# Group averages on the vector engine by 32x32 block transposes, from the fourth sample on

## The reference

```
# per sample; x, ctx: 256 x 1024; 8 groups of 32 rows ("GROUPS = 8", cg = 32)
t = Wt @ ctx;  p = Wp @ layernorm(x);  g = Wg @ ctx
att = sum over each group (32 rows x 1024) of p * g          # one number per group
y  = Wz_group @ (att * t)                                    # per group, 32 x 32
yn = (y - mean(y)) * rsqrt(var(y) + 1e-5)                    # mean, var over the group
x  = x + tanh(g_xattn) * (yn * gn_w + gn_b + ctx)
# feed-forward: h = layernorm(x)
scores = (h @ Wq^T) @ keys^T                                 # 64 experts, rank 8 each
gate   = softmax over the 16 largest scores, 0 elsewhere
out    = ((h @ A^T) * gate, each gate over 8 columns) @ B^T * 2
x      = x + tanh(g_ffn) * out
```

## Time and profile before

| | us |
|---|---|
| median of 3 runs | 324.51 (324.15 to 326.56) |
| the profiled execution, its own time | 325.73 |
| its span, first to last instruction | 323.9 |
| PE busy | 319.0 (98%) |
| DVE busy | 245.9 (76%) |
| ACT busy | 174.9 (54%) |
| POOL busy | 168.5 (52%) |
| mean granted clock of TensorE | 0.995 of full |

### The profile page before, as it was taken

How to read it: one execution, slowest core, us unless ns; L and a number is a source line. 1 busy time by engine, 2 the same in 40 slices (tenths; PEclk the granted TensorE clock), 3 DMA queues, 4 the chain that set the end, 5 groups by cost and what they waited for, 6 DMA issues and landing times.

```text
span 323.9 us, 5543 instructions
## 1 busy us (share of the span) xinstructions
PE 319.0 (98%) x1960; PEld 290.4 (90%) x1960; DVE 245.9 (76%) x636; ACT 174.9 (54%) x298; POOL 168.5 (52%) x158
## 2 busy tenths in 40 slices
PE   8999999999999999999999999999999999999996
PEld 6688998899988999898999899898999889989985
DVE  1856897596588946888887799788987798789362
ACT  3687845677256485286545658177454654354110
POOL 0464699189463969339581677429591580010000
PEclk9998999999999999999999999999999999999999
DMA  7999900990650585249951899228961631272102
GB/s 248 412 388 397 363 4 7 328 306 10 191 200 13 184 300 190 63 134 272 405 200 34 253 358 361 67 89 275 365 252 61 224 134 74 58 244 82 65 32 99
DMA packets 28091, 62.69 MB, mean 194 GB/s; under 512 B 2448, under 2 KB 12560, under 8 KB 28064
## 3 DMA queue, kind: packets, MB, share of 16 engines
q1 hardware_dynamic: 27712, 62.14, 54.6%
q10 hardware_dynamic: 352, 0.20, 0.2%
HBM read 46.34 MB, written 15.99 MB: 192 GB/s over the span
## 4 chain that ended last, share of the span: by engine, by line
PE 94%; DMA 3%; SPq 1%; issue 0%; ACT 0%; DVE 0%
PE z_ps L1266 20%; PE w_ps L1296 18%; PE w_ps L1185 12%; PE w_ps L1266 12%; PE z_ps L1125 9%; PE w_ps L1303 9%; PE z_ps L1104 4%; DMA cT_first<-in_cT 3%; PE t_ps L1213 2%; PE w_ps L1125 2%; PE t_ps L1243 2%; PE t_ps L1280 1%; PE z_ps L1198 1%; PE z_ps L1213 1%; PE t_ps L1342 1%; PE w_ps L1314 0%
## 5 line engine op out<-in xcount | busy, mean ns | idle before, releaser
L1296 PE MATMUL w_ps<-B_hi,zT_hi 128*128 128x512 f32 x124 | 49.3, 397 | 0.0
L1296 PE MATMUL w_ps<-B_lo,zT_hi 128*128 128x512 f32 x124 | 48.4, 391 | 0.0
L384 POOL TENSOR_TENSOR xT_lo<-xT_in,xT_hi 128x512 fp32r<-128x512 f32 x24 | 30.6, 1298 | 20.5 <-ACT xT_hi L500 17.7
L418 POOL TENSOR_TENSOR c_sb<-c_sb,x_sb 128x512 f32<-128x512 f32 x28 | 36.2, 1329 | 6.9 <-ACT c_sb L603 6.9
L403 POOL TENSOR_TENSOR c_lo<-c_sb,c_hi 128x512 fp32r<-128x512 f32 x24 | 30.3, 1292 | 14.1 <-DVE uw L863 14.1
L557 ACT ACTIVATE uw<-w_ps,neg_u 128x512 f32<-128x512 f32 x32 | 20.2, 686 | 28.8 <-DVE neg_u L808 28.8
L574 ACT ACTIVATE hT_hi<-t_ps 128x512 fp32r<-128x512 f32 x32 | 18.5, 599 | 30.7 <-DVE t_ps L884 22.5
L1266 PE MATMUL z_ps<-A_hi,hT_hi 128*128 128x288 f32 x160 | 34.7, 298 | 0.2 <-ACT hT_hi L574 0.2
L1266 PE MATMUL z_ps<-A_lo,hT_hi 128*128 128x288 f32 x160 | 34.1, 294 | 0.0
L1303 PE MATMUL w_ps<-B_hi,zT_lo 128*128 128x512 f32 x124 | 33.3, 390 | 0.0
L384 POOL TENSOR_TENSOR cT_lo<-cT_in,cT_hi 128x512 fp32r<-128x512 f32 x24 | 30.6, 1300 | 2.4 <-DVE uw L863 2.4
(11 more groups left out here) (191 smaller groups left out, 846.8 us busy)
## 6 DMA issues: line engine op xcount, KB each, us to landing
c_sb<-in_ctx SPq DMA_DIRECT2D x16, 512.0 KB, 6.8
x_sb<-in_x SPq DMA_DIRECT2D x16, 512.0 KB, 7.3
xT_in<-in_xT SPq DMA_DIRECT2D x14, 512.0 KB, 6.8
cT_in<-in_cT SPq DMA_DIRECT2D x14, 512.0 KB, 8.1
out_block<-uw SPq DMA_DIRECT2D x14, 512.0 KB, 6.2
w_through<-uw SPq DMA_DIRECT2D x10, 512.0 KB, 3.2
c_sb<-w_through SPq DMA_DIRECT2D x10, 512.0 KB, 4.0
z_through<-zg_sb SPq DMA_DIRECT2D x9, 256.0 KB, 2.3
```

What stands on the lines that cost most here:

```text
L384: last = pool.tensor_tensor(lo[:, chunks, :], came[:, chunks, :], hi[:, chunks, :].bitcast(f32), ALU.subtract)
L418: last = pool.tensor_tensor(c_sb[n % 2][:, t, cols], c_sb[n % 2][:, t, cols], x_sb[:, t, cols], ALU.add)
L1296: pe.matmul(w_ps[k][:, :], zT_hi[:, t, row], w[:, j, cols], start=(j == 0 and w is B_hi), stop=False)
```

## The change

For samples 0 to 2 nothing changes in the order of the work. From sample 3 on (samples 3 to 7) both averages over the groups are made on DVE, by a new helper of three instructions, each waiting for the one before: a transpose of a 128x32 tile in blocks of 32x32, so that each group's 32 values of one column lie along one row; a product with ones and 1/32 with a running sum, which leaves the average of each row in one column; and a transpose of that column, read 32 times over, which puts it back into all rows of the group. The inputs `u_mv` and `att_var` become the first columns of zeroed 128x32 tiles. The ten small products on PE, the copy of their result out of PSUM, and PE's waits for them are gone.

```diff
+        u_block, att_block = sb("u_block", [P, GROUP]), sb("att_block", [P, GROUP])
+        u_mv = u_block[:, 0:2 * T].rearrange("p (t k) -> p t k", k=2)
+        turned_in, turned_out, ones = sb("turned_in", [P, GROUP]), sb("turned_out", [P, GROUP]), sb("ones", [P, GROUP])
+        group_avg = sb("group_avg", [P, 1])
-        att_var, va = sb("att_var", [P, 2 * T]), sb("va", [P, 2 * T])
+        att_var, va = att_block[:, 0:2 * T], sb("va", [P, 2 * T])
...
+            def averages(block):
+                step(dve.transpose(turned_in[:, :], block[:, :]))
+                settle()
+                step(dve.scalar_tensor_tensor(turned_in[:, :], turned_in[:, :], 1.0 / GROUP, ones[:, :],
+                                              ALU.mult, ALU.mult, accum_out=group_avg[:, :]))
+                settle()
+                return dve.transpose(turned_out[:, :], group_avg[:, :].to_broadcast([P, GROUP]))
             def group_deviation(n):
-                dve.wait_ge(mean_sum, n + 1)
-                dve.tensor_tensor(u_dev[:, :], u_mv[:, :, 0], t_ps[1][:, 0:T], ALU.subtract).then_inc(mean_read, 1)
+                if n < 3:
+                    dve.wait_ge(mean_sum, n + 1)
+                    means = t_ps[1][:, 0:T]
+                else:
+                    step(averages(u_block))
+                    settle()
+                    means = turned_out[:, 0:2 * T].rearrange("p (t k) -> p t k", k=2)[:, :, 0]
+                dve.tensor_tensor(u_dev[:, :], u_mv[:, :, 0], means, ALU.subtract).then_inc(mean_read, 1)
...
             def slopes(n, meanwhile=None):
-                dve.wait_ge(va_sum, n + 1)
-                dve.tensor_copy(va[:, :], t_ps[1][:, 0:2 * T]).then_inc(va_read, 1)
+                if n < 3:
+                    dve.wait_ge(va_sum, n + 1)
+                    dve.tensor_copy(va[:, :], t_ps[1][:, 0:2 * T]).then_inc(va_read, 1)
+                    of = va
+                else:
+                    dve.wait_ge(u_rows, per_tile(n, T - 1))
+                    dve.wait_ge(att_rows, per_tile(n, T - 1))
+                    averages(att_block).then_inc(va_read, 1)
+                    of = turned_out
                 dve.wait_ge(va_read, n + 1)
...
+            step(dve.memset(u_block[:, :], 0.0))
+            step(dve.memset(att_block[:, :], 0.0))
+            step(dve.memset(ones[:, :], 1.0))
...
-                    gram(m + 1, {(0, 3): lambda: group_means(m), (0, 6): lambda: group_att_var(m),
-                                 (1, KH): lambda: ctx_sums(m + 1)})
+                    gram(m + 1, {(1, KH): lambda: ctx_sums(m + 1)})
...
-                    z_product(1, b, {(1, 0): lambda: group_means(m), (KH - 1, 0): lambda: group_att_var(m)})
+                    z_product(1, b)
```

More of the change, by code:

```diff
@@ L87, in flamingo_block @@
         c_sum, beta = sb("c_sum", [P, T]), sb("beta", [P, T])
-        u_st, u_mv, neg_u = sb("u_st", [P, T, NH * 6]), sb("u_mv", [P, T, 2]), sb("neg_u", [P, T])
+        u_st, neg_u = sb("u_st", [P, T, NH * 6]), sb("neg_u", [P, T])
+        u_block, att_block = sb("u_block", [P, GROUP]), sb("att_block", [P, GROUP])
+        u_mv = u_block[:, 0:2 * T].rearrange("p (t k) -> p t k", k=2)
+        turned_in, turned_out, ones = sb("turned_in", [P, GROUP]), sb("turned_out", [P, GROUP]), sb("ones", [P, GROUP])
+        group_avg = sb("group_avg", [P, 1])
         w_sq, w_ve, w_rs = sb("w_sq", [P, T]), sb("w_ve", [P, T]), sb("w_rs", [P, T])
         u_dev = sb("u_dev", [P, T])
-        att_var, va = sb("att_var", [P, 2 * T]), sb("va", [P, 2 * T])
+        att_var, va = att_block[:, 0:2 * T], sb("va", [P, 2 * T])
         att, a2 = sb("att", [P, T]), sb("a2", [P, T])
@@ L831, in slopes @@
             def slopes(n, meanwhile=None):
-                dve.wait_ge(va_sum, n + 1)
-                dve.tensor_copy(va[:, :], t_ps[1][:, 0:2 * T]).then_inc(va_read, 1)
+                if n < 3:
[7 more added lines that the diff above has]
+                    of = turned_out
                 dve.wait_ge(va_read, n + 1)
-                step(dve.scalar_tensor_tensor(a2[:, :], va[:, 0:T], float(GROUP * GROUP), va[:, 0:T],
+                step(dve.scalar_tensor_tensor(a2[:, :], of[:, 0:T], float(GROUP * GROUP), of[:, 0:T],
                                               ALU.mult, ALU.mult))
-                step(dve.scalar_tensor_tensor(att[:, :], va[:, 0:T], float(GROUP), gnw_t[:, :],
+                step(dve.scalar_tensor_tensor(att[:, :], of[:, 0:T], float(GROUP), gnw_t[:, :],
                                               ALU.mult, ALU.mult))
@@ L840, in slopes @@
                 for t in range(T):
-                    last = dve.tensor_scalar(y_ve[:, t:t + 1], a2[:, t:t + 1], va[:, T + t:T + t + 1], EPS,
+                    last = dve.tensor_scalar(y_ve[:, t:t + 1], a2[:, t:t + 1], of[:, T + t:T + t + 1], EPS,
                                              ALU.mult, ALU.add)
```

## The result

| | runs | median us | lowest to highest |
|---|---|---|---|
| before | 20 | 324.65 | 324.07 to 326.56 |
| changed | 20 | 326.19 | 325.90 to 328.06 |

The ratio changed to before is 1.0047, with a 95% interval of 1.0031 to 1.0062: about 1.5 us slower, 1.0 to 2.0. That is under 1%, as forecast, and in the range of 323.6 to 327.3; the point forecast of 325.5 was 0.7 short. The direction was right. At full clock the change costs 1.68 us (326.10 against 324.42; for before, whose clocks are not on record here, the 11 runs under 325 us).

What follows compares the result with a forecast made beforehand. DVE's chain to hT_hi, not busy PE, was taken to bound: 0.47 us delay less 0.27 slack, four times 0.20, plus 0.21 at the last sample, +1.0 us, median 324.51 to 325.5; range 323.6 to 327.3.

Steps and rivals of the forecast that it cites:

- What bounds it: PE is 94% of the span, but its saving counts only as far as the DVE and ACT chain to z_product(0, m) allows.
- The price of a small product on PE: Each small product costs PE 0.23 us; two per sample over samples 3 to 7 give a ceiling of 2.3 us gain.
- The transpose: On DVE, a 32-column transpose takes 213 ns, from a line between 154 ns and 1124 ns; upper value 275 ns.
- The delay of the chain: On DVE, u_dev comes 0.24 us later and the slope 0.47 us later in samples 3 to 6.
- arrives in full: On the path from the averages to hT_hi no wait takes up delay, so all that DVE adds reaches the end.
- The slack at hT_hi: Ahead of z_product(0, m), 0.27 us of the 0.42 distance is free; 0.15 by the load of weights.
- the price of a stalled start: When PE waits for hT_hi, release costs 0.04 us and the first pair of products 0.11 us more, together 0.15.
- Idle time of PE: Before z_product(0, 3) to (0, 6), PE idles about 0.6 us per sample, together with smaller waits earlier.
- Sample 3: Like samples 4 to 6: chain 0.47 us later less 0.27 slack, so z_product(0, m) starts 0.20 us later.
- Sample 7: Chain 0.28 us later through w and gate(1, 6), against 0.07 slack before zT(1, 6): +0.21 us.
- Rival 1: Averages on DVE are cheap and PE keeps part of its gain: 324.3 us, down to 322.2; chance 0.25.
- rival 2: Slower by over 1%: small transposes on DVE take over about 0.325 us; at 0.40 us, 329.3 us; chance 0.08.

Runs made afterwards that it cites:

- e1: Changed kernel with the ten small products issued again on PE, their result read by nobody; 326.67 us, ratio 1.0058 to before.
- e2: Changed kernel with both averages left out from sample 3 on (ones for the means, a copy for the second); 323.46 us, ratio 0.9950 to before.
- e10: Changed kernel with one six-column average on DVE, x_moments(m + 1) ahead of the last statistics, ctx_sums three products later; 322.32 us, ratio 0.9930 to before.
- e8: Kernel before with one small six-column product on PE instead of two, no transposes; 323.42 us, ratio 0.9963 to before.
- e4: Kernel before with four small dependent DVE instructions (0.80 us) ahead of the slope in samples 3 to 7; 327.53 us, ratio 1.0087 to before.
- e5: Changed kernel with x_moments(m + 1) moved behind zT_turn(1, b) on DVE and POOL's root of them moved likewise; 330.58 us, ratio 1.0192 to before.
- e6: Changed kernel with one average of six columns on DVE instead of two of two and four; 323.55 us, ratio 0.9966 to before.
- e3: Kernel before with one small dependent DVE instruction (0.20 us) ahead of the slope in samples 3 to 7; 324.93 us, ratio 1.0003 to before.
- e7: e6 plus e5's move of x_moments and POOL's root, and ctx_sums three products later in gram; 326.69 us, ratio 1.0061 to before.
- e9: Changed kernel with x_moments(m + 1) moved ahead of the last statistics, u_statistics(m, (0,)), on DVE; 326.13 us, ratio 1.0033 to before.

## Why the prediction was right, and where its sizes were off

**What bounds it.** Right, and it was the point that decided: PE at 94% of the chain did not mean that PE's saving counts. e1 gives PE the work back and the turn doesn't change; e2 and e10 take the delay away and it does.

**The price of a small product on PE, 0.23.** Right: e8 removes one and gains 0.22.

**The transpose, 213 ns.** Right. The changed kernel's groups on DVE (busy us, mean ns of one | idle before):

```profile
L833 DVE STREAM_TRANSPOSE turned_out<-group_avg 128x32 f32<-128x32 f32 x10 | 2.1, 211 | 0.3
L830 DVE SCALAR_TENSOR_TENSOR turned_in<-turned_in,ones 128x32 f32<-128x32 f32 x10 | 1.9, 192 | 0.3
L828 DVE STREAM_TRANSPOSE turned_in<-att_block 128x32 f32<-128x32 f32 x5 | 1.0, 208 | 0.0
L828 DVE STREAM_TRANSPOSE turned_in<-u_block 128x32 f32<-128x32 f32 x5 | 1.0, 201 | 0.0
```

201 to 211 ns, also where one column is read 32 times. The straight line between 154 ns for one column and 1124 for 512 held. The Trainium skill, "VectorE: DVE Perf Modes", section "The TRN2 errata — SBUF-src ops pay a fixed extra latency per instruction", had two answers: the estimated 94 ns of its table is contradicted by these rows, the estimated 190 ns of its measured fixed part is near them.

**The delay of the chain.** Predicted 0.24 at u_dev, measured 0.22; predicted 0.47 at the slope, measured 0.44. Up to hT_hi, from the same statistics, it is 16.49 against 16.09: 0.40. So a little of the delay, 0.04, is lost on the way, which "arrives in full" had excluded. The step was right in kind and 0.07 too large.

**The slack at hT_hi, taken as 0.27.** Too large, by about as much. (The distance of 0.42 that it starts from is 0.40 at sample 5, not within 0.01.) The term that was mis-sized is the price of a stalled start, put at 0.04 + 0.11 from the one case of before. In the changed kernel it is 0.14 from the end of hT_hi to the first product (189.95 to 190.09) and 0.09 in the pair, 0.23 together; 0.42 - 0.23 = 0.19, as in e4. By the load of weights the prediction had 0.15 as the other end; the measured 0.19 lies between the two, and I took an end. Two errors of 0.06 to 0.08 with opposite effect left the net per turn, +0.20, where it was predicted: 0.19, 0.21 and 0.22 for samples 4 to 6.

**Idle time of PE, "about 0.6 per sample".** Right as a balance: 0.46 + 0.20 lost in each turn. By parts (sample 4, against before): PE reaches ctx_sums 24.54 us behind z_product(0, 3) instead of 24.82, so 0.18 of the 0.46 is gone there already: 0.10 as in e2, where ctx_sums comes too early for c_hi, and 0.08 by the slower restart of z_product(0, 3). From there it takes 0.48 longer: 0.05 in ctx_sums (0.43 instead of 0.38) and 0.42 at z_product(0, 4), of which 0.26 is shown as a wait for hT_hi and 0.16 is the overlap that is lost. Whoever looks in the list of waits for 0.6 finds less than half of it.

**Sample 3.** Missed: its turn is longer by 0.41, not 0.20. Its hT_hi is late by 0.68 instead of 0.40, and the 0.28 are a gap in the changed kernel's DVE, between the averages:

```profile
137.67 0.20 DVE L768 BATCH_NORM_AGGREGATE x_mv<-x_st 128x2 f32<-128x12 f32 x1
138.03 0.21 DVE L768 BATCH_NORM_AGGREGATE x_mv<-x_st 128x2 f32<-128x12 f32 x1 [0.16 <-issue]
```

In all other samples the second of these follows the first at once (0.27 for both, here 0.57). The transposes don't make the gap: e1, e2, e5, e6 and e10 have one of 0.23 to 0.29 in the same sample too, and e2 has no transposes. In e2 it stands ahead of another instruction:

```profile
138.51 0.17 DVE L857 COPY va<-att_block 128x4 f32<-128x4 f32 x1 [0.19 <-issue]
```

In all six it is the same place in the queue, ahead of DVE's 320th instruction of the trace, its waits counted. In before, e3, e4, e7, e8 and e9, where another instruction stands at that place, there is none. What the engine does in the gap stays open. Without it the turn would be longer by 0.13 and not by 0.20, as no slower restart comes before it.

**Sample 7.** Predicted +0.21, measured +0.27, of which 0.07 is the slower restart of z_product(0, 6) at the turn's own beginning; the prediction had charged that to sample 6. What belongs to sample 7 is 0.20. Its two terms were about right: the chain is 0.27 later (from the last statistics to the gate's product 10.13 us instead of 9.86; 0.28 predicted), and the slack is then 0.07, as predicted, where e3 and e4 give 0.04. The two rows of the changed kernel (answering to the earlier trace rows):

```profile
288.25 0.88 DVE L959 SCALAR_TENSOR_TENSOR zg_sb<-z_ps,g_scale,eg 128x288 f32<-128x288 f32 x2
...
289.18 0.75 PE L1310 MATMUL t_ps<-ident,zg_sb 128*128 128x128 f32 x4 [0.61 <-DVE zg_sb L959]
```

PE starts 0.05 behind the gate's end, but its four small products take 0.75 instead of 0.63.

**The sum.** Predicted 4 x 0.20 + 0.21 = 1.01; in the profile 1.30. Sorted by cause that is 0.13 + 0.19 + 0.21 + 0.22 + 0.07 = 0.82 for the four starts of z_product(0, 3) to (0, 6), 0.20 for sample 7, and 0.28 for the gap, of which the kernel before shows no sign. The runs show 1.5, at full clock 1.68, with the 0.3 outside the span, which the prediction did not have either and which stays open. **Rival 1** fell with the transposes at 0.21 and the slack below my value; **rival 2** fell with the transposes too. "The changed profile shows 37.2 instead of 37.0" is what it shows for three samples of four.

**The base.** The median of before was 324.51 in 3 runs and 324.65 in 20. That the profiled execution lay 1.2 above was put down to nothing in particular; it was its clock near the start (3.4 us at half the clock, below), an estimated 1.7 us.

## What to carry to other kernels

An engine that is 94% of the chain need not be the one whose work counts: look for the one place per turn where its input comes from elsewhere, read how long before its need that input is ready, take off the price of a stalled start (here 0.23 of 0.42 us), and compare with the delay that the change puts on that path. Work may leave the busy engine for free only as far as this slack goes; a second edit that makes room on the path (moments into an idle gap, one average instead of two, a reader of a fresh result one step later) turned +1.5 us into -2.0. And when an instruction is moved on one engine, follow its reader's queue: behind a waiting x_root of 0.7 us on POOL stood 5 us of other work, and behind that ACT's part of the chain.

## What the runs showed of the hardware

- In four of the twelve profiles (before, e1, e2, e9) the granted clock is 0.50, the lower of TensorE's two levels (1.2 GHz), for 3.4 us near the start, and 1.00 in the rest of the span from there; in the other eight this stretch is missing. In before it lies at about 24.0 to 27.4 us. This is its line of granted clock in 40 slices, with the 8 in the fourth:

```profile
PEclk9998999999999999999999999999999999999999
```

- After a wait for ACT, PE started 0.14 us behind the end of the activation where the stationary operand had to be loaded first, and its first pair of products took 0.09 longer; after DVE's gate it started after 0.05 and lost 0.12 in the four products. Together that is 0.17 to 0.23 us for being just too late, and 0.07 to 0.08 of it reaches the next statistics.
- A 32-column transpose on DVE takes 201 to 211 ns from SBUF to SBUF, a 512-column one with a strided output into PSUM 1112 to 1166 (means of the changed kernel's two groups).
- A gap marked "issue", which sets DVE back by 0.23 to 0.29 us, stands ahead of DVE's 320th instruction in six of the twelve profiles, whatever that instruction is.
